# A decoder layer on one core: squares, the bias of the attention output, the experts' product and the last chunk's passes are rearranged

## The chip, the cores and the metric

The kernel runs on one NeuronCore of a Trainium2 chip. The metric is the device time of one launch, in microseconds (us). The core has a tensor engine for matmuls (PE, with PEld for its weight loads), a vector engine (DVE), a scalar engine (ACT), GpSimd (POOL) and a sync engine (SP), which here issues all DMAs. Each engine runs its own instruction list in order; semaphores tie them together. A later instruction on an engine can't pass one that waits.

## The reference

All arrays are float32: x is 4 x 1024 x 512, the context 4 x 64 x 512. One layer has three blocks, each added to its input and followed by a LayerNorm:

```python
# block 1: state-space mixer and gated MLP
h  = x + mamba(rmsnorm(x) * w1)      # in_proj 512->2048, conv of 4 taps, silu, x_proj,
                                     # dt = softplus(...), h[t] = exp(dt*A)*h[t-1] + dt*B*u (16 states),
                                     # y = (C.h + D*u) * silu(z), out_proj 1024->512
xn = rmsnorm(h) * w2
b1 = h + (silu(xn @ w1.T) * (xn @ w2.T)) @ w3.T          # width 2048
x  = layernorm(x + b1)
# block 2: cross attention to 64 context keys, 16 heads
scores = q.k / sqrt(32)
t = exp(clip(mlp(mean of scores, mean row maximum, mean variance of softmax)))   # per head, over the sequence
out = softmax(q.k / (2 t)) @ v
x = layernorm(x + out @ Wo.T + bo)
# block 3: a dense product with experts of low rank
base = x @ W.T + b
gate = softmax(x @ R.T), kept for its top 2 of 8 experts, rescaled to sum 1
h = x @ A.T                          # 8 experts x 16 = 128 columns
x = layernorm(x + base + (gate * h) @ B)
```

The temperature t of a batch needs statistics over its whole sequence of 1024, so the attention proper of a batch can only begin when both of its halves have passed the first scores.

## The kernel before, in words

The 4 sequences are cut into 8 chunks of 512 tokens (c = 0 to 7; an even chunk and the next odd one make a sequence). The work of a chunk is cut into units, and five streams of units are laid over each other:

- **m, the mixer.** Its front for a chunk: `turn_in` (normalise and transpose the input), `conv` (input product and convolution, 8 blocks), `proj`, the first `dt` and softplus steps. Its scan: 64 steps; in each, GpSimd multiplies by B (L992) and later by C (L1002) on 128x1024 elements, ACT computes two decays (L1049), DVE runs two scans (L1339), and the sum over states goes to PE (L1644, half of it to DVE). After the scan come `gate`, `out` (the output product, 32 matmuls, L1589), `ht` (residual, squares for the second norm), `rms` and `turn_out` (normalised and transposed into the tile `fT`, L1600).
- **l**, the gate branch z and the later dt blocks.
- **y**, the dense part of block 1: `h`/`hv`/`hg`/`hm` (gated MLP, 16 blocks), `w3`, its LayerNorm, `turn` (transposed into `fT`) and `query`, which reads `fT`.
- **s**, the statistics: `sc1` (scores of 128 tokens and 8 heads, L1677), `mx` (row maximum, DVE L1428), `e1` (8 exponentials, ACT L1220, then a square L1224), `sq` (DVE L1434), `ent`; at an odd chunk `mean`, `mlp`, `clip`, `temper`. There are 8 of these groups per chunk.
- **x**, the pass of a chunk through blocks 2 and 3: four times (t = 0 to 3) `sc2`, `e2` (ACT L1254), `flip` (transposes, L1704, copied by ACT L1263), `val` (L1711), `on` (DVE L1481), `fl2` (L1717, ACT L1268), `wo` (output product, L1542, with a bias product L1723 ahead of it), `woa` (DVE L1485); then LayerNorm, `xturn` (L1656), `lg` and `hh` (16 small products each), `logits`/`top2` (a chain of small DVE operations), `gh`, `lora`, `base` with `fin` (L1740, L1542, L1753), `mixed`, LayerNorm.

Which unit comes next on an engine is decided when the program is built: `schedule` lists the units by a greedy walk with durations per unit (`m_parts`, `parts`), and among the heads of the five streams it takes the one that could start first; within a stream's look-ahead (`LOOK`) it takes the one with the smaller key, which is set by `PHASE`, one number per stream and chunk. `loads` places the DMAs on SP's list by the same walk. The list is fixed from then on: where the chip is later than the walk, engines wait in the written order. The 8 PSUM banks are shared: banks 0 to 3 serve the mixer and are given free for the other streams after the last `turn_out`, banks 4 to 7 serve the rest.

Three waits matter below. ACT writes the squares of `ht` into `fT`, which the `query` products of the chunk before read, so `ht` waits for all four of them. The weights of `wo` and of `base` share one tile pair `watt`, loaded in turns. And the passes of the chunks are one list: no unit of pass 7 stands ahead of any unit of pass 6 on any engine.

In the text, "scan c" runs on GpSimd from the first multiplication of chunk c (its `du`, L1017) to its last product by C, and "front c" from there to the start of scan c+1. Front 7 is what follows the last scan.

## Time and profile before

| | us |
|---|---|
| median of 3 timed runs | 4170.89 |
| lowest, highest | 4154.61, 4172.75 |
| time of the profiled execution | 4160.77 |
| its span | 4159.0 |
| PE busy | 3674.8 (88%) |
| POOL busy | 2441.5 (59%) |
| DVE busy | 2519.4 (61%) |
| ACT busy | 2165.4 (52%) |
| span after the last `out` begins (3574.8) | 584.2 |

Times in rows count from the start of the span. A busy PE isn't PE at its peak, since its matmuls are pipelined and their ends are modelled; one float32 matmul stands as two records. "<-" names what ended the idle time before an instruction. TensorE's granted clock stands as a share of 2.4 GHz, averaged over a stretch. A row on a stretch A:B gives its length and then the busy time (and number of instructions) of PE, PEld, DVE, ACT and POOL, the granted clock, the busy share of the DMA engines and GB/s.

### The profile page before, as it was taken

What the parts mean: (1) busy time and instruction counts of PE and PEld (TensorE: products, weight loads), DVE (VectorE), ACT (ScalarE), POOL (GpSimd) and SP (SyncE); (2) the same over time, 40 slices, a digit from 0 to 9 for tenths busy, and PEclk for the clock granted to TensorE, in tenths of its full rate; (3) what the DMA queues carried; (4) which work ended last, traced back from release to release, by engine and by line L of the source; (5) the groups of instructions that cost most, each with busy time, mean ns of one, the idle gap of its engine ahead of it and who ended that gap; (6) DMA issues with size and microseconds to landing.
All of it is one profiled execution on the core that took longest, in us unless ns stands there. A gap on an engine that the chain in (4) does not pass through costs nothing.

```text
span 4159.0 us, 36287 instructions
## 1 busy us (share of the span) xinstructions
PE 3674.8 (88%) x9984; PEld 1760.8 (42%) x9984; DVE 2519.4 (61%) x3286; ACT 2165.4 (52%) x5182; POOL 2441.5 (59%) x1069
## 2 busy tenths in 40 slices
PE   7667998899879999999989998999989998999477
PEld 3223443444334445544434345554334434554244
DVE  4884678567746886168755887158774787222211
ACT  5543544554555455565456547455466457340543
POOL 3884599559954995049963997029981998100000
PEclk9889999899989999999989999999989999999788
DMA  4433344335433442235433442125432443112000
GB/s 171 138 121 101 120 164 162 97 115 167 149 106 117 158 156 74 86 112 168 152 111 104 157 159 97 66 83 187 152 128 82 157 162 119 49 46 91 11 31 21
DMA packets 221268, 483.19 MB, mean 116 GB/s; under 512 B 31884, under 2 KB 32268, under 8 KB 220812
## 3 DMA queue, kind: packets, MB, share of 16 engines
q1 hardware_dynamic: 221068, 480.87, 35.5%
q8 instruction: 83, 1.36, 0.1%
q14 instruction: 117, 0.96, 0.1%
HBM read 470.82 MB, written 9.96 MB: 116 GB/s over the span
## 4 chain that ended last, share of the span: by engine, by line
PE 58%; POOL 7%; ACT 6%; DVE 6%; issue 5%; POOLq 0%; DVEq 0%; ACTq 0%
PE ps L1542 32%; PE ps L1629 7%; PE ps L1644 6%; PE ps L1589 5%; POOL hb L1002 5%; DVE hb L1339 2%; POOL hb L992 2%; PE ps L1677 2%; PE ps L1711 1%; ACT ps L1220 1%; ACT xw L1254 1%; PE ps L1723 1%; PE ps L1582 1%; PE ps L1753 1%; PE ps L1740 1%
## 5 line engine op out<-in xcount | busy, mean ns | idle before, releaser
L1002 POOL TENSOR_TENSOR hb<-hb,bc 128x1024 f32<-128x1024 f32 x512 | 1224.5, 2394 | 96.8 <-issue 53.2
L992 POOL TENSOR_TENSOR hb<-dtu,bc 128x1024 f32<-128x1024 f32 x481 | 1133.2, 2357 | 124.3 <-PE ps L1644 85.6
L1049 ACT ACTIVATE ps<-dt,a_neg 128x512 f32<-128x512 f32 x1024 | 697.3, 690 | 841.1 <-DVE hb L1339 834.8
L1542 PE MATMUL ps<-fT,wden 128*128 128x512 f32 x2304 | 1038.5, 599 | 10.0 <-DVE hm L1392 6.7
L1644 PE MATMUL ps<-hb,ident 128*128 128x512 f32 x1152 | 653.2, 668 | 255.7 <-POOL hb L1002 254.3
L1542 PEld LDWEIGHTS ps<-fT,wden 128*128 128x128 f32 x2304 | 441.1, 193 | 568.4 <-issue 568.1
L1339 DVE TENSOR_TENSOR_SCAN hb<-ps,state,hb 128x512 f32<-128x512 f32 x512 | 626.6, 1266 | 19.2 <-POOL hb L992 12.9
L1339 DVE TENSOR_TENSOR_SCAN hb<-ps,hb 128x512 f32<-128x512 f32 x512 | 593.8, 1204 | 17.0 <-POOL hb L992 12.4
L1355 DVE TENSOR_TENSOR ps<-ps,hb 128x512 f32<-128x512 f32 x448 | 311.0, 694 | 274.1 <-POOL hb L1002 273.3
L1629 PE MATMUL ps<-wden,hm 128*128 128x512 f32 x1024 | 469.7, 606 | 1.5 <-DVE res L1402 1.5
L1542 PE MATMUL ps<-xnT,wmix 128*128 128x512 f32 x1024 | 456.9, 595 | 13.8 <-ACT xnT L1073 7.8
L1644 PEld LDWEIGHTS ps<-hb,ident 128*128 128x128 f32 x1152 | 218.1, 205 | 590.0 <-POOL hb L1002 401.1
L1017 POOL TENSOR_TENSOR dtu<-dt,u 128x1024 f32<-128x1024 f32 x32 | 75.4, 2358 | 629.5 <-issue 559.6
L1629 PEld LDWEIGHTS ps<-wden,hm 128*128 128x128 f32 x1024 | 198.9, 195 | 258.6 <-issue 247.0
L1542 PEld LDWEIGHTS ps<-xnT,wmix 128*128 128x128 f32 x1024 | 193.7, 191 | 251.8 <-issue 251.5
L1025 POOL TENSOR_TENSOR res<-bc,res 128x512 f32<-128x512 f32 x32 | 39.5, 1266 | 319.9 <-DVE bc L1376 319.9
L1589 PE MATMUL ps<-wmix,u 128*128 128x512 f32 x512 | 221.4, 593 | 5.4 <-DVE u L1361 5.3
L1254 ACT ACTIVATE xw<-ps,nm,ftv 128x64 f32<-128x64 f32 x512 | 199.2, 421 | 20.4 <-PE ps L1677 20.4
L1306 DVE SCALAR_TENSOR_TENSOR hb<-hb,cols 128x512 f32<-128x512 f32 x192 | 143.9, 750 | 36.5 <-ACT hb L1092 31.9
L1402 DVE TENSOR_TENSOR res<-ps,res 128x512 f32<-128x512 f32 x128 | 86.7, 680 | 114.9 <-PE ps L1629 114.3
L1171 ACT ACTIVATE hm<-ps 128x512 f32<-128x512 f32 x128 | 75.0, 587 | 153.7 <-PE ps L1542 96.4
L1589 PEld LDWEIGHTS ps<-wmix,u 128*128 128x128 f32 x512 | 96.9, 190 | 128.7 <-issue 128.7
(197 smaller groups left out, 3980.5 us busy)
## 6 DMA issues: line engine op xcount, KB each, us to landing
bc<-bc_dram SPq DMA_DIRECT2D x1024, 256.0 KB, 3.6
wden<-in_w SPq DMA_DIRECT2D x192, 512.0 KB, 3.6
wmix<-in_w_mix SPq DMA_DIRECT2D x96, 512.0 KB, 3.7
watt<-in_w_qof SPq DMA_DIRECT2D x32, 512.0 KB, 4.3
xm<-in_x SPq DMA_DIRECT2D x8, 1024.0 KB, 5.5
res<-in_x SPq DMA_DIRECT2D x8, 1024.0 KB, 6.9
wden<-in_w_qof SPq DMA_DIRECT2D x16, 512.0 KB, 3.6
out<-res SPq DMA_DIRECT2D x8, 1024.0 KB, 4.3
```

Source lines behind the costliest of these rows:

```text
L992: TTn(hb[:, k % 4], dtu[:, :, :], bc[:, 0, k % 3].unsqueeze(1).broadcast_to([P, 2, CH]), ALU.mult).then_inc(s.s1_ready, 1)
L1002: TTn(hb[:, k % 4], hb[:, k % 4], bc[:, 1, k % 3].unsqueeze(1).broadcast_to([P, 2, CH]), ALU.mult).then_inc(s.s3_done, 1)
L1049: A_(dst, dt[:, p % 2, jj], ACT.Exp, scale=a_neg[:, j, n:n + 1]).then_inc(full_of(key), 1)
L1254: ins = A_(eb[:, hh], bank[:, h], ACT.Exp, bias=nm2[:, TT * half + i, hh:hh + 1], scale=ftv[:, 0, hh:hh + 1], accum_out=den[:, 0, i % 2, h ...
L1306: ins = V.scalar_tensor_tensor(acc[:, j % 3], up[:, j % 2, tap:tap + CH], conv_w[:, j, tap:tap + 1], acc[:, j % 3], ALU.mult, ALU.add)
L1339: V.tensor_tensor_scan(hb[:, i % 4, jj], src, hb[:, i % 4, jj], first, ALU.mult, ALU.add).then_inc(free_of(key), 1)
L1355: V.tensor_tensor(ps[:, 2], ps[:, 2], hb[:, i % 4, 0], ALU.add).then_inc(s.sum_done, 1)
L1402: V.tensor_tensor(res[:, c % 3, tt], src, res[:, c % 3, tt], ALU.add).then_inc(free_of(key), 1)
L1542: ins = M(dst, a, b, start=start and n == 0, stop=stop and n == len(pairs) - 1)
L1589: ins = M(dst[t], u[:, j, t * P:(t + 1) * P], wo, start=j == 0, stop=j == JB - 1)
L1629: ins = M(dst, hm[:, f, tt * P:(tt + 1) * P], wi[:, (f % 2) * 512:(f % 2) * 512 + 512], start=f == 0, stop=f == FG - 1)
L1644: ins = M(dst, ident[:, :], hb[:, i % 4, jj], start=False, stop=n == NS - 1)
```

## The change

1. **Squares.** ACT writes them into `xnT` and no longer waits for the queries of the chunk before; that wait moves to `turn_out`, which writes `fT`.
2. **Last chunk.** The passes of chunk 7 become a stream of their own, `w`, so that its units may stand between those of pass 6. The `base` weights of passes 6 and 7 are loaded once into `u`, whose mixer data is no longer needed, and pass 7 uses the `wo` weights of pass 6. In those two passes all four `base` products stand ahead of `lora`.
3. **Experts.** `hh` is computed transposed: 4 matmuls with 512 moving columns in place of 16 with 128. So DVE first copies the gates out 16-fold (a new 128x512 copy), PE transposes them (`lora`), and `gh` multiplies the transposed product.
4. **Bias.** The bias product ahead of each `wo` (32 in all) is gone. GpSimd adds the bias to the residual in a new unit `bo`, 4 additions of 128x512 per chunk; `bo` of chunk c-1 stands behind `ht` of chunk c on GpSimd, and `woa` waits for it. One more constant is loaded at the start.
5. **Values.** The attention values have one buffer in place of two, with a semaphore of their own.
6. The planner's durations, waits, `PHASE` and `LOOK` are new, so that units move on every engine.

Cut to its core:

```diff
-    got = [("out", c, 0), ("ht", c, 0), ("ht", c, 1), ("ht", c, 2), ("ht", c, 3)]
+    got = [("out", c, 0), ("ht", c, 0), ("ht", c, 1), ("ht", c, 2), ("ht", c, 3)] + ([("bo", c - 1)] if c else [])
...
-        got += [("hh", c), ("gh", c), ("lora", c), ("base", c, 0)]
+        early = 0 if c < CHUNKS - 2 else 4
+        got += [("hh", c)] + [("base", c, t) for t in range(early)] + [("lora", c), ("gh", c)]
         for t in range(TT):
-            got += [("fin", c, t), ("mixed", c, t)] + ([("base", c, t + 1)] if t + 1 < TT else [])
+            got += ([("base", c, t)] if t >= early else []) + [("fin", c, t), ("mixed", c, t)]
...
+            part(ACT_, EV, mine(n), ("query", c - 1, KC - 1))
+    elif kind == "bo":
+        part(POOL, 5.2, ("turn", c, KC - 1))
     elif kind == "out":
         for p in range(PAIRS):
             part(PE, 8 * MM, ("gate", c, PAIRS - 1))
     elif kind == "ht":
         part(DVE, EV, ("out", c, 0), ("store", c - 3), late=7.0 if c > 2 else 0.0)
-        part(ACT_, 0.9, mine(0), ("query", c - 1, KC - 1))
+        part(ACT_, 0.9, mine(0))
...
-WORK = {"x": 176.0, "s": 103.0, "y": 304.0}
-PHASE = {'y': (6.12, 6.01, 6.206, 6.132, 6.127, 6.01, 6.132, 6.01), 's': (7.437, 6.89, 7.686, 6.881, 7.587, 6.627, 6.484, 6.736), 'x': (8.786, 7.926, 8.998, 8.055, 8.453, 7.926, 9.282, 7.057)}
+WORK = {"w": 176.0, "x": 176.0, "s": 103.0, "y": 304.0}
...
-        got[("wf", c)] = ("wo", c, TT - 1)
+        got[("wf", c)] = ("wo", c, TT - 1) if c < CHUNKS - 2 else ("out", CHUNKS - 1, 0)
...
-    streams = {"m": m_plan(), "l": l_plan(), "x": x_plan(), "s": s_plan(), "y": y_plan()}
+    streams = {"m": m_plan(), "l": l_plan(), "x": x_plan(range(CHUNKS - 1)), "w": x_plan((CHUNKS - 1,)), "s": s_plan(), "y": y_plan()}
...
-LOOK = {'m': 0.162, 'l': 0.065, 'x': 0.046, 'y': 0.288, 's': 0.3}
+LOOK = {'w': 0.05, 'm': 0.265, 'l': 0.167, 'x': 0, 'y': 0.277, 's': 0.3}
...
+        if c < CHUNKS - 1:
+            got.append((DONE[("fin", c - 1, TT - 1)] if c else 0.0, 2, ("wo_load", c)))
+            got.append((DONE[("wo", c, TT - 1) if c < CHUNKS - 2 else ("out", CHUNKS - 1, 0)], 2, ("wf_load", c)))
...
+    got.append((kept + 6, 2, ("v_load", 0)))
+    for b in range(1, BATCH):
+        got.append((DONE[("val", 2 * b - 1, TT - 1)], 2, ("v_load", b)))
...
-        vbd = sb("vbd", [P, 2, HEADS // 2, 2 * DK])
+        vbd = sb("vbd", [P, HEADS // 2, 2 * DK])
...
+        def gh_of(c):
+
+            g = hm[:, 0] if c == CHUNKS - 2 else xw[:, 0:512]
+            return g.rearrange("p (t c) -> p t c", t=TT)
+
+        def ghT_of(c):
+            return hm[:, 1] if c == CHUNKS - 2 else xw[:, 512:1024]
...
+                if c == CHUNKS - 2:
+                    filled(sp, ("out", CHUNKS - 1, TT - 1))
+                    for m in range(2):
+                        sp.dma_start(u[:, 2 * m:2 * m + 2].rearrange("p j l -> p (j l)"), A["w_qof"][4 + m]).then_inc(s.wu_in, 16)
+                    return
...
-                    filled(sp, ("val", 2 * b - 3, TT - 1))
                     sp.wait_ge(s.kb_sum, b - 1)
                 for q in range(4):
                     sp.dma_start(kbd[32 * q:32 * q + 32, r, :, q * KEYS:(q + 1) * KEYS],
                                  k_dram[b, :, 32 * q:32 * q + 32, :].rearrange("c p k -> p c k")
                                  ).then_inc(kv_in[r], 16)
+
+            def load_v(b):
+                sp.wait_ge(s.zeroed, 2)
+                if b:
+                    filled(sp, ("val", 2 * b - 1, TT - 1))
                 vv = v_dram[b].rearrange("k (a e d) -> k a e d", e=2, d=DK)
                 for e in range(2):
-                    sp.dma_start(vbd[64 * e:64 * e + 64, r, :, DK * e:DK * e + DK], vv[:, :, e, :]
-                                 ).then_inc(kv_in[r], 16)
+                    sp.dma_start(vbd[64 * e:64 * e + 64, :, DK * e:DK * e + DK], vv[:, :, e, :]).then_inc(v_in, 16)
...
+                elif kind == "bo":
+                    pool.wait_ge(s.const_in, 16 * CONSTS)
+                    for c4 in range(KC):
+                        filled(pool, ("tr", c, 0, c4))
+                    for t in range(TT):
+                        ins = TTn(res[:, c % 3, t], res[:, c % 3, t], bo_b[:, :], ALU.add)
+                    ins.then_inc(s.bo_in, 1)
...
-                    if i == 0 and c:
-
-                        for c4 in range(KC):
-                            filled(act, ("q", c - 1, c4))
-                    A_(fT[:, i], ht[:, i], ACT.Square, accum_out=smo[:, 0, i:i + 1]).then_inc(s.ss2_ready, 1)
+                    if c == CHUNKS - 1 and i == 0:
+                        filled(act, ("z", c, JB - 1))
+                    A_(xnT[:, i], ht[:, i], ACT.Square, accum_out=smo[:, 0, i:i + 1]).then_inc(s.ss2_ready, 1)
...
+                    for c4 in range(KC) if c else ():
+                        filled(act, ("q", c - 1, c4))
...
+                    dve.wait_ge(s.bo_in, c + 1)
...
-                        V.tensor_tensor(gates, G1, each(gmax[:, :]), ALU.mult).then_inc(free_of(("lg", c)), 1)
+                        ch.link(V.tensor_tensor(gates, G1, each(gmax[:, :]), ALU.mult))
+                        V.tensor_copy(gh_of(c).rearrange("p t (e r) -> p t e r", e=EXPERTS), bcast(gates, RANK)
+                                      ).then_inc(free_of(("lg", c)), 1)
                 elif kind == "gh":
                     key = ("hh", c)
-                    emptied(dve, ("lg", c))
-                    h = filled(dve, key).rearrange("p (t e r) -> p t e r", t=TT, e=EXPERTS)
-                    V.tensor_tensor(gh.rearrange("p t (e r) -> p t e r", e=EXPERTS), h, bcast(gate[:, 2], RANK), ALU.mult
-                                    ).then_inc(free_of(key), 1)
+                    emptied(dve, ("lora", c))
+                    V.tensor_tensor(ghT_of(c), filled(dve, key), ghT_of(c), ALU.mult).then_inc(free_of(key), 1)
...
-                    M(dst, e64[:, :], w_dt[:, 0:512], start=True, stop=False)
-                    group(dst, [(oT[:, c4 * P:(c4 + 1) * P], wo[c4 // 2][:, c4 % 2]) for c4 in range(KC)], start=False
-                          ).then_inc(full_of(unit), 1)
-                elif kind in ("lg", "hh"):
+                    group(dst, [(oT[:, c4 * P:(c4 + 1) * P], wo[c4 // 2][:, c4 % 2]) for c4 in range(KC)]).then_inc(full_of(unit), 1)
+                elif kind == "lg":
                     for c4 in range(KC):
                         emptied(pe, ("tr", c, 1, c4))
                     dst = take(pe, unit)
-                    wide, at_ = (EXPERTS, 0) if kind == "lg" else (P, EXPERTS)
                     for t in range(TT):
                         T = TT * half + t
-                        ins = group(dst[:, t * wide:(t + 1) * wide],
-                                    [(qT[:, ci, T * P:(T + 1) * P], w_ra[:, ci, at_:at_ + wide]) for ci in range(KC)])
+                        ins = group(dst[:, t * EXPERTS:(t + 1) * EXPERTS],
+                                    [(qT[:, ci, T * P:(T + 1) * P], w_ra[:, ci, 0:EXPERTS]) for ci in range(KC)])
                     ins.then_inc(full_of(unit), 1)
+                elif kind == "hh":
+                    group(take(pe, unit), [(w_ra[:, ci, EXPERTS:RA], qT[:, ci, half * CH:(half + 1) * CH]) for ci in range(KC)]
...
+                    if c < CHUNKS - 2:
+                        wb = x_in(pe, 2 * c + 1)
+                    else:
+                        pe.wait_ge(s.wu_in, 32)
+                        wb = [u[:, 2 * m:2 * m + 2].rearrange("p j (c d) -> p (j c) d", d=DM) for m in range(2)]
...
-                    emptied(pe, ("hh", c))
+                    emptied(pe, ("lg", c))
                     for t in range(TT):
-                        ins = turn(dst[:, t * P:(t + 1) * P], gh[:, t], ident[:, :])
+                        ins = turn(dst[:, t * P:(t + 1) * P], gh_of(c)[:, t], ident[:, :])
...
-                        emptied(pe, ("lora", c))
-                    M(ps[:, USE[key][0]], ghT[:, i * P:(i + 1) * P], w_b[:, :], start=False, stop=True
+                        emptied(pe, ("hh", c))
```

`CONSTS` goes from 14 to 15, the tile `bo_b` (128x512) and the semaphores `bo_in`, `wu_in` and `v_in` are added, and the waits for `val`, `fl2` and `wo` in the first of the four steps are now also made against the pass before.

Three places on PE show what the new tables do. The first is behind `out` of chunk 5, between scans 5 and 6. L1589 is `out`, L1559 `turn_in` of chunk 6 (L1624 and L1594 after); L1704, L1717 and L1711 are flips and values, L1677 scores, L1542 with fT the queries, with watt the attention's output product. Before:

```order
L1589 MATMUL ps<-wmix,u 128x512 x32
L1704 MATMUL ps<-ident,xw 128x128 x8
L1677 MATMUL ps<-kbd,qT 128x256 x2
L1711 MATMUL ps<-vbd,xw 128x64 x8
L1677 MATMUL ps<-kbd,qT 128x256 x2
L1542 MATMUL ps<-fT,wden 128x512 x4
L1717 MATMUL ps<-ident,xw 128x128 x4
L1542 MATMUL ps<-fT,wden 128x512 x4
L1723 MATMUL ps<-w_dt,e 128x512
L1542 MATMUL ps<-watt,xw 128x512 x4
L1704 MATMUL ps<-ident,xw 128x128 x8
L1677 MATMUL ps<-kbd,qT 128x256 x2
```

and now:

```order
L1624 MATMUL ps<-wmix,u 128x512 x32
L1739 MATMUL ps<-ident,xw 128x128 x8
L1712 MATMUL ps<-kbd,qT 128x256 x2
L1747 MATMUL ps<-vbd,xw 128x64 x8
L1712 MATMUL ps<-kbd,qT 128x256 x4
L1753 MATMUL ps<-ident,xw 128x128 x4
L1712 MATMUL ps<-kbd,qT 128x256 x2
L1577 MATMUL ps<-watt,xw 128x512 x4
L1712 MATMUL ps<-kbd,qT 128x256 x2
L1739 MATMUL ps<-ident,xw 128x128 x8
L1712 MATMUL ps<-kbd,qT 128x256 x2
L1594 MATMUL ps<-dgi,xm 128x128 x16
```

Before, 28 rows stand between `out` and `turn_in`; now the three queries and one of the four attention steps stand ahead of `out`, and the last two steps behind `turn_in`.

The second is the end of the last chunk's MLP: L1629 is `w3`, L1677 with two or more matmuls the scores of the statistics, L1656 the transposes, L1542 with fT the MLP and the queries, L1687 the statistics' end. Before:

```order
L1629 MATMUL ps<-wden,hm 128x512 x16
L1542 MATMUL ps<-fT,wden 128x512 x24
L1677 MATMUL ps<-kbd,qT 128x256 x2
L1629 MATMUL ps<-wden,hm 128x512 x16
L1677 MATMUL ps<-kbd,qT 128x256 x4
L1656 MATMUL ps<-ident,res 128x128 x16
L1542 MATMUL ps<-fT,wden 128x512 x16
L1677 MATMUL ps<-kbd,qT 128x256 x16
```

and now (L1664 is `w3`, L1712 the scores, L1691 the transposes):

```order
L1664 MATMUL ps<-wden,hm 128x512 x16
L1577 MATMUL ps<-fT,wden 128x512 x24
L1712 MATMUL ps<-kbd,qT 128x256 x2
L1664 MATMUL ps<-wden,hm 128x512 x16
L1712 MATMUL ps<-kbd,qT 128x256 x14
L1691 MATMUL ps<-ident,res 128x128 x16
L1577 MATMUL ps<-fT,wden 128x512 x16
L1712 MATMUL ps<-kbd,qT 128x256 x16
```

Before, five of chunk 6's eight score groups stand further up, among the attention steps of pass 5; now all eight stand at the end, seven of them behind the last `w3`.

The third is where pass 6 ends. L1711 are values, L1656 transposes, L1542 with w_ra `lg` and `hh`, L1747 `lora`, the rest `base` and `fin`. Before:

```order
L1717 MATMUL ps<-ident,xw 128x128 x4
L1723 MATMUL ps<-w_dt,e 128x512
L1542 MATMUL ps<-watt,xw 128x512 x4
L1656 MATMUL ps<-ident,res 128x128 x16
L1542 MATMUL ps<-w_ra,qT 128x8 x16
L1542 MATMUL ps<-w_ra,qT 128x128 x16
L1747 MATMUL ps<-ident,xw 128x128 x4
L1740 MATMUL ps<-w_dt,e 128x512
L1542 MATMUL ps<-watt,qT 128x512 x4
L1753 MATMUL ps<-w_b,xw 128x512
L1740 MATMUL ps<-w_dt,e 128x512
L1542 MATMUL ps<-watt,qT 128x512 x4
```

and now (L1577 with watt and xw is `wo`, L1739 flips of pass 7, L1691 the transposes of pass 6, L1780 and L1577 with u `base` of pass 6):

```order
L1577 MATMUL ps<-watt,xw 128x512 x4
L1739 MATMUL ps<-ident,xw 128x128 x4
L1691 MATMUL ps<-ident,res 128x128 x16
L1739 MATMUL ps<-ident,xw 128x128 x4
L1712 MATMUL ps<-kbd,qT 128x256 x2
L1577 MATMUL ps<-w_ra,qT 128x8 x16
L1577 MATMUL ps<-qT,w_ra 128x512 x4
L1780 MATMUL ps<-w_dt,e 128x512
L1577 MATMUL ps<-u,qT 128x512 x4
L1780 MATMUL ps<-w_dt,e 128x512
L1577 MATMUL ps<-u,qT 128x512 x4
L1780 MATMUL ps<-w_dt,e 128x512
```

Before, pass 7 begins behind all of pass 6; now its first step runs between `wo` and the LayerNorm of pass 6, and `lg`, `hh` and all four `base` products of pass 6 stand inside its second step, ahead of that step's `val`.

## Rows read from the trace of the kernel before

**Rows 1.** The page, its first part: busy time by engine.

```profile
PE 3674.8 (88%) x9984; PEld 1760.8 (42%) x9984; DVE 2519.4 (61%) x3286; ACT 2165.4 (52%) x5182; POOL 2441.5 (59%) x1069
```

**Rows 2.** Stretches: length, busy time by engine, granted clock, DMA.

```profile
457.40:782.00 324.60, 284.78 (x633) 121.12 (x631) 253.49 (x284) 159.12 (x266) 305.76 (x132) 0.93 0.46 150
...
1301.00:1645.70 344.70, 318.70 (x899) 152.87 (x898) 264.96 (x332) 193.79 (x382) 306.12 (x132) 0.95 0.43 138
1645.70:1824.90 179.20, 169.37 (x594) 93.54 (x593) 57.31 (x116) 97.05 (x320) 4.96 (x5) 0.97 0.22 71
...
2151.20:2254.40 103.20, 93.41 (x269) 47.32 (x268) 46.16 (x76) 66.46 (x220) 4.92 (x4) 0.97 0.27 88
2254.40:2598.90 344.50, 317.87 (x897) 152.11 (x896) 265.88 (x331) 193.93 (x382) 306.08 (x132) 0.95 0.43 138
2598.90:2782.90 184.00, 174.22 (x595) 98.05 (x594) 57.42 (x116) 97.03 (x320) 4.95 (x5) 0.94 0.22 69
2782.90:3108.00 325.10, 301.40 (x690) 131.13 (x689) 253.76 (x307) 179.28 (x374) 305.87 (x132) 0.95 0.47 154
...
3210.70:3553.80 343.10, 318.56 (x901) 152.79 (x900) 266.76 (x331) 191.33 (x373) 306.04 (x132) 0.96 0.43 139
```

**Rows 3.** Timeline of PE around the `out` of chunks 4 and 5.

```profile
2154.61 27.70 PE L1589 MATMUL ps<-wmix,u 128*128 128x512 f32 x64 [0.91 <-DVE u L1361]
2191.09 5.83 PE L1559 MATMUL ps<-dgi,xm 128*128 128x128 f32 x32 [5.33 <-ACT dgi L1069]
...
2621.34 27.63 PE L1589 MATMUL ps<-wmix,u 128*128 128x512 f32 x64
...
2696.21 3.79 PE L1559 MATMUL ps<-dgi,xm 128*128 128x128 f32 x32
```

**Rows 4.** The chain that ended last: bias, four matmuls, `lg` with `hh`.

```profile
3628.63 0.86 PE ps L1723 x2
3629.49 3.43 PE ps L1542 x8
...
4008.51 10.65 PE ps L1542 x64
```

**Rows 5.** Stretches after the last `out` begins, columns as in rows 2.

```profile
3574.80:3861.00 286.20, 283.10 (x838) 145.49 (x837) 63.04 (x124) 92.27 (x317) 4.94 (x4) 0.98 0.19 65
...
3861.00:3892.50 31.50, 21.18 (x65) 12.07 (x65) 7.94 (x19) 16.35 (x54) 0.00 (x0) 0.89 0.06 17
3892.50:3941.90 49.40, 9.95 (x68) 8.30 (x67) 14.33 (x33) 30.74 (x151) 0.00 (x0) 0.60 0.00 0
3941.90:3997.00 55.10, 45.37 (x180) 29.21 (x179) 6.13 (x12) 33.15 (x141) 0.00 (x0) 0.84 0.00 1
3997.00:4048.60 51.60, 37.27 (x140) 24.70 (x140) 14.49 (x49) 12.22 (x19) 0.00 (x0) 0.84 0.12 41
4048.60:4102.40 53.80, 42.02 (x176) 26.33 (x176) 5.84 (x11) 34.45 (x142) 0.00 (x0) 0.84 0.05 20
4102.40:4159.00 56.60, 35.55 (x133) 23.18 (x132) 14.78 (x49) 12.19 (x18) 0.00 (x0) 0.81 0.10 37
```

**Rows 6.** Timeline of ACT: first and last statistics group of chunk 7.

```profile
3892.54 0.21 ACT L1216 ACTIVATE nm<-mxs 128x8 f32<-128x8 f32 x1 [2.12 <-DVE mxs L1428]
...
3926.35 0.21 ACT L1216 ACTIVATE nm<-mxs 128x8 f32<-128x8 f32 x1 [1.35 <-DVE mxs L1428]
```

**Rows 7.** Timeline of DVE: `woa` of two steps of pass 6.

```profile
3962.14 0.69 DVE L1485 TENSOR_TENSOR res<-ps,res 128x512 f32<-128x512 f32 x1 [6.80 <-PE ps L1542]
...
3972.86 0.69 DVE L1485 TENSOR_TENSOR res<-ps,res 128x512 f32<-128x512 f32 x1 [6.05 <-PE ps L1542]
```

**Rows 8.** Groups by line and shape: additions on GpSimd.

```profile
L1025 POOL TENSOR_TENSOR res<-bc,res 128x512 f32<-128x512 f32 x32 | 39.5, 1266 | 319.9 <-DVE bc L1376 319.9
```

**Rows 9.** DVE's multiplications in scan 0: least, median, most ns.

```profile
L1346 DVE TENSOR_TENSOR hb<-dtu,bc x31: 1198/2035/3411, 83.0 to 350.9; 128x1024 f32<-128x1024 f32 x31
```

**Rows 10.** The page, DMA issues: a row spread over 128 partitions.

```profile
bc<-bc_dram SPq DMA_DIRECT2D x1024, 256.0 KB, 3.6
```

76 lines of the change are left out of this document (40 added, 36 removed).

## The prediction, made before the changed kernel had run

> **What bounds the kernel now.** I read the busy times first: PE 88%, no other engine above 61% [rows 1]. An average hides stages, so I cut the span at the mixer's borders, where GpSimd starts and stops its steps [rows 2]. In each scan GpSimd is busy for 306 us. Scans 1 and 6 last 324.6 and 325.1 us, so GpSimd bounds them. Scans 3, 5 and 7, in which PE also does most of an attention pass, last 343 to 345 us with PE busy for 318: there PE's written order makes GpSimd wait for its sums. Fronts come in two kinds. Front 4 takes 103.2 us with PE busy for 93.4. Fronts 3 and 5 take 179.2 and 184.0 with PE busy for 169.4 and 174.2: they carry another pass, ahead of the mixer on PE. The timeline shows it: `turn_in` starts 8.8 us after `out` ends in front 4 (2154.61 + 27.70 to 2191.09), but 47.2 us after it in front 5 (2621.34 + 27.63 to 2696.21) [rows 3].
>
> After the last `out` begins, 584.2 us remain [rows 5]: 286.2 bound by PE (283.1 busy); 31.5 of LayerNorm and queries; 49.4 of statistics, in which PE works for 10; pass 6 with 55.1 for its four attention steps and 51.6 for the rest; pass 7 with 53.8 and 56.6. In these last four PE is busy for 37 to 45 us each, ACT for 12 to 34. No engine bounds them; a chain does. One attention step takes 10.7 us (`woa` at 3962.14 and 3972.86 [rows 7]), because its flips stand behind the `wo` of the step before and each link waits for the last.
>
> **The change part by part.** Prices of PE: a bias matmul takes 0.86 us, four matmuls of 512 columns 3.43, and `lg` with `hh`, 32 small products, 10.65, so half of it, 5.3, for `hh` [rows 4].
>
> *Bias and experts.* Each chunk loses 4 x 0.86 = 3.4 us of bias and 5.3 - 3.4 = 1.9 of `hh`, together 5.3 of PE. Five passes lie before the last `out`, so 26.5 us of PE work go there. GpSimd gains four additions of 1.27 us [rows 8], 5.1 per chunk. They stand right behind `ht`, where GpSimd idles for some 60 us until the next scan (its 4.92 busy of 103.2 in front 4 is `ht` alone [rows 2]): nothing on the path. If that cover were gone, 6 x 5.1 = 31 us. The new copy of the gates is one DVE operation per chunk, as wide as `woa` at 0.69 [rows 7]; DVE is busy for 61% of the span, and in the two last passes the four `base` products run meanwhile: nothing.
>
> *Fronts.* Front 3 has, besides 1.9 for `hh` and three bias groups (2.6), three queries (10.3) and one attention step (about 9.5 with its bias, by the prices above and the small products) fewer: 24 us, and PE is busy for 169 of its 179, so -24. In front 5 `turn_in` moves up past two steps and the queries: about 16 us instead of 47.2 behind `out`. The path behind it took 2254.40 - 2191.09 = 63.3 us in front 4 and 86.7 in front 5; with two attention steps still woven in I take 75, and 12 ahead of `out`. 12 + 27.6 + 16 + 75 is 131, and with some waiting 134: -50.
>
> *Scans.* What left the fronts is in the scans. Counting units at the prices above: scan 3 gets 15 us of PE work more, scan 5 15 more (both net of the bias), scan 6 18.6 more (the rest of pass 3, 20 us of `base` in one block between two sums, against MLP blocks that moved into front 5), scan 7 5.3 less. Nothing in the trace shows these orders, so I bound the price of 1 us of PE work moved into a scan. From below 0: scan 1 with 285 busy and scan 6 with 301 last equally long. From the rows nearest to it: scan 6 to scan 5 adds 16.5 busy and 19.4 of length, 1.2 per us. Scans 3 and 5 are past the bend, scan 6 stands just before it. I take 1: +49, and -5 for scan 7. Together with the fronts -24 - 50 + 49 - 5 = -30; ends: -79 and, at 1.5 per us, -5.
>
> *Front 7 up to the last `w3`.* PE-bound, so work counts: bias 3.4, `hh` 1.9, five score groups moved behind it (0.88 each by PE's 0.86 for the same number of columns, 4.4). -10, with 3 us of idle time as the other bound: -7 to -13. Here the squares no longer wait for the last query. That is worth little beyond this: PE was idle for 3.1 of 286.2 us, so the wait was covered by other products. The same holds for the other fronts.
>
> *Statistics of chunk 6.* The part of the change that costs. One group of statistics takes 4.83 us ((3926.35 - 3892.54)/7 [rows 6]), since maximum, exponentials, square and sum go to and fro between DVE and ACT. Before, five of the eight ran beside the attention steps of pass 5, which cost nothing. Now seven start behind the last `w3`. Between there and the end of the queries (31.5 us) about four fit, as ACT also has 16 us of its own work there less what it already did for two groups; flips of the transposes wait behind them and delay the queries by 2. The other four are 3.7 x 4.83 = 18, so chunk 7's statistics start 20 us later: +20. Bounds: 0 if they all fitted, 5 x 4.83 = 24 if none of the moved ones did.
>
> *Last passes.* Pass 6's four steps lose a bias each and share ACT with the first exponentials of pass 7: 55.1 - 3.4 + 1.7 = 53.4. Then, from its last `wo`: the first step of pass 7 (10.7); a second step that takes PE's block of pass 6, `xturn` 3.4 (as many columns as four matmuls of 512), `lg` 5.3, `hh` 3.4, `base` 17.2, `fin` 3.4, so about 45; and two steps of some 11.5 (9.9 without the bias, and ACT's scaling and table changes between). 10.6 + 45 + 23 = 78.6. The end is as before but for 1: 55.5. Sum 187.5 against 217.1: -30. Bounds: 0, if the block of pass 6 cost as much as its LayerNorm chain did (51.6 + 53.8 = 105.4 for both), and -51.6, if all of it were hidden.
>
> *The rest.* One more constant, 3.6 us as a lone transfer [rows 10], shares the queues with the others: +1, at most +3.6. The values in one buffer are needed only at the next sequence's first step: 0.
>
> Sum: -30 - 10 + 20 - 30 + 1 = -49, from 4160.8 to 4112 for an execution like the profiled one. The median of the timed runs stands 10.1 above that execution; I put in half and forecast 4118.
>
> **A rule against the change.** DVE's multiplication of two SBUF operands in scan 0 takes 1.20 us alone, but 2.04 in the median and up to 3.41 beside GpSimd's products [rows 9]: one waits for the other. The Trainium skill, "SBUF — State Buffer", section "SBUF: two separate sides", says that such a DVE operation and a GpSimd operation take one shared port pair in turn, each for the whole instruction; by that rule the trace agrees. New here are eight DVE copies within SBUF, four or more of them in scans, and 32 GpSimd additions. By rows 9 a collision costs at most 3.41 - 1.20 = 2.2 us: eight copies give 18 us, and the additions, which stand ahead of the convolution's taps, none. I leave it out of the sum and keep it as a rival.
>
> **The rivals.**
> - *The moved work isn't absorbed.* A 20 us block between two sums outlasts the four buffers that GpSimd works ahead (4 steps of 306/64 = 4.8 us, 19 us), and scans 3 and 5 now hold queries too. Scan 7 already ends so. At 1.6 to 1.8 per us the scans give +78 to +88 instead of +49: 4150.
> - *Pass 7 stands behind pass 6's block.* If its second step takes 65 instead of 45: 4138. For it: PE's order is fixed; against it: that step's own chain is only 10.
> - *Port waits*, as above, all eight and in the path: 4136.
> - *More than forecast.* Scan 6 takes its 18.6 us within its 24 us of idle PE, and front 5 goes to front 4's length: 4085.
> - *Slower than before.* One mechanism: GpSimd's products stop while PE does attention blocks in scans 3, 5 and 6. The other terms add up to -98 (-24, -50, -5, -10, +20, -30, +1); it decides from 98/49 = 2.0 us per us moved. At 2.5 the sum is +24: 4190. For it: the waits of the flips for ACT's exponentials stop PE as well, which a count of work doesn't contain. Against it: the 1.2 of the nearest rows.
>
> **How the numbers follow.** Forecast 4118 with its own range of 4098 to 4140: 0.58. Moved work not absorbed, 4150: 0.16. Pass 7 behind the block, 4138: 0.08. Port waits, 4136: 0.05. More, 4085: 0.07. Slower: 0.06. The range that holds 8 in 10 is 4085 to 4155. Less than 0.5%, 21 us, can't be told from no change. Faster means below 4150: 0.58 + 0.08 + 0.05 + 0.07 and a third of the 0.16, 0.83; the same 0.11, and slower 0.06.
>
> **What would show it.** Front 5 near 134 us with `turn_in` about 16 behind `out`; front 3 near 155; scans 3 and 5 near 360, scan 6 near 343, scan 7 near 338; the even fronts and scans 1, 2 and 4 unchanged; the last `out` beginning near 3545; 276 us from there to the last `w3`; chunk 7's first statistics 51 us behind it (31.5 before); then 49 to the first exponentials of pass 6, and 187 from there to the end, with one step of pass 7 of about 45 us. I am wrong if scan 6 grows by more than 30, if the statistics of chunk 6 cost nothing, or if the last two passes together save less than 15.

## The result and the profile after the change

The changed kernel takes 4145.32 us in the median of 8 runs (4136.56 to 4146.62), the kernel before 4167.0 in 8 runs beside it; the ratio is 0.9947 (95% interval 0.9935 to 0.9958). It is faster by 22 us, 0.5%, less than half of the 49 in the prediction's sum. The profiled executions differ by 17.9 us in span (4141.1 against 4159.0).

The page's busy times (span, then each engine's busy time and share) answer to [rows 1]: GpSimd has the additions, PE has lost only 1% and is still the busiest.

```profile
span 4141.1 us, 35899 instructions
PE 3648.7 (88%) x9728; PEld 1712.2 (41%) x9728; DVE 2527.0 (61%) x3294; ACT 2173.9 (52%) x5187; POOL 2481.8 (60%) x1101
```

The stretches of scans and fronts, with the columns of [rows 2]: scan 3, front 3, scan 5, front 5, scan 6, scan 7.

```profile
1299.30:1678.20 378.90, 350.72 (x961) 165.31 (x961) 273.82 (x347) 212.24 (x437) 306.18 (x132) 0.95 0.40 132
1678.20:1823.50 145.30, 133.79 (x475) 72.97 (x475) 54.43 (x107) 88.09 (x304) 9.87 (x9) 0.96 0.22 72
2256.50:2634.00 377.50, 349.99 (x962) 164.92 (x961) 273.82 (x347) 212.42 (x437) 306.15 (x132) 0.96 0.41 132
2634.00:2758.10 124.10, 113.99 (x395) 61.62 (x394) 43.49 (x67) 78.97 (x274) 9.87 (x9) 0.97 0.22 74
2758.10:3110.10 352.00, 324.08 (x762) 141.86 (x760) 266.21 (x342) 184.01 (x368) 306.23 (x132) 0.93 0.44 144
3212.60:3564.00 351.40, 321.66 (x878) 151.19 (x877) 269.48 (x333) 191.30 (x373) 306.35 (x132) 0.95 0.41 136
```

Against [rows 2] the fronts fell by 33.9 and 59.9 us, and the scans grew by 34.2, 33.0, 26.9 and 8.3. PE's busy time tells the same: 35.6 and 60.2 us left the two fronts, 32.0, 32.1, 22.7 and 3.1 arrived in the scans. The last `out` begins at 3580.84, 6 us later than before, where the prediction had it 30 earlier.

Behind it the stretches are: from the last `out` to the last `w3`; from there to the sums of chunk 7's statistics; from there to the end. In the kernel before, whose `out` begins at 3574.65 and whose sums at 3935.27, the same three took 286.4, 74.3 and 223.7 us. The first row here is that of the sums before (L1687), the others are the three stretches now:

```profile
3935.27 0.94 PE L1687 MATMUL ps<-ones_t,sta 128*3 128x1 f32 x32 [37.45 <-DVE sta L1457]
3580.80:3850.30 269.50, 268.99 (x786) 132.95 (x785) 56.77 (x115) 74.74 (x225) 9.85 (x8) 1.00 0.22 73
3850.30:3945.30 95.00, 35.59 (x108) 21.36 (x108) 27.66 (x56) 59.82 (x288) 4.93 (x4) 0.68 0.02 6
3945.30:4141.10 195.80, 152.35 (x606) 91.96 (x606) 42.93 (x127) 94.49 (x325) 0.00 (x0) 0.86 0.03 11
```

So +6.2 up to the last `out`, then -16.9, +20.7 and -27.9. Behind the last `out` the forecast (-10, +20, -30) holds for the two later stretches and is 7 us short of what the first one saved; before the last `out` it fails.

### The profile page after: what moved, and what is told of

The parts are those of the page before. It is cut to its first block, busy times and chain, and to the rows that moved or that the text cites. A ratio compares the mean times of both kernels' runs of the same rounds, so it can differ in the third digit from the quotient of the medians.

```text
span 4141.1 us, 35899 instructions
## 1 busy us (share of the span) xinstructions
PE 3648.7 (88%) x9728; PEld 1712.2 (41%) x9728; DVE 2527.0 (61%) x3294; ACT 2173.9 (52%) x5187; POOL 2481.8 (60%) x1101
## 4 chain that ended last, share of the span: by engine, by line
PE 56%; POOL 7%; ACT 7%; DVE 6%; issue 5%; POOLq 0%; DVEq 0%; ACTq 0%
PE ps L1577 31%; PE ps L1664 7%; PE ps L1679 6%; POOL hb L1027 5%; PE ps L1624 5%; DVE hb L1373 2%; POOL hb L1017 2%; PE ps L1712 1%; ACT xw L1288 1%; PE ps L1747 1%; ACT ps L1252 1%; PE ps L1617 1%; PE ps L1793 1%; PE ps L1780 1%; PE ps L1594 1%
## 5 line engine op out<-in xcount | busy, mean ns | idle before, releaser
L1577 PE MATMUL ps<-fT,wden 128*128 128x512 f32 x2304 | 1042.7, 601 | 16.1 <-DVE hm L1426 6.7
L1577 PEld LDWEIGHTS ps<-fT,wden 128*128 128x128 f32 x2304 | 442.0, 193 | 577.5 <-issue 573.4
L1373 DVE TENSOR_TENSOR_SCAN hb<-ps,hb 128x512 f32<-128x512 f32 x512 | 593.6, 1204 | 12.5 <-POOL hb L1017 9.0
L1664 PE MATMUL ps<-wden,hm 128*128 128x512 f32 x1024 | 470.5, 606 | 2.1 <-DVE res L1436 1.9
L1577 PE MATMUL ps<-xnT,wmix 128*128 128x512 f32 x1024 | 456.7, 596 | 13.6 <-ACT xnT L1105 8.2
L1664 PEld LDWEIGHTS ps<-wden,hm 128*128 128x128 f32 x1024 | 198.7, 195 | 260.2 <-issue 246.8
L1577 PEld LDWEIGHTS ps<-xnT,wmix 128*128 128x128 f32 x1024 | 193.9, 191 | 253.6 <-issue 253.3
L1624 PE MATMUL ps<-wmix,u 128*128 128x512 f32 x512 | 221.4, 593 | 6.1 <-DVE u L1395 6.1
L1288 ACT ACTIVATE xw<-ps,nm,ftv 128x64 f32<-128x64 f32 x512 | 199.3, 421 | 17.0 <-PE ps L1712 16.7
L1053 POOL TENSOR_TENSOR res<-res,bo_b 128x512 f32<-128x512 f32 x32 | 39.5, 1270 | 241.8 <-PE ps L1691 241.8
```

The source lines that it names most:

```text
L1288: ins = A_(eb[:, hh], bank[:, h], ACT.Exp, bias=nm2[:, TT * half + i, hh:hh + 1], scale=ftv[:, 0, hh:hh + 1], accum_out=den[:, 0, i % 2, h ...
L1373: V.tensor_tensor_scan(hb[:, i % 4, jj], src, hb[:, i % 4, jj], first, ALU.mult, ALU.add).then_inc(free_of(key), 1)
L1577: ins = M(dst, a, b, start=start and n == 0, stop=stop and n == len(pairs) - 1)
L1624: ins = M(dst[t], u[:, j, t * P:(t + 1) * P], wo, start=j == 0, stop=j == JB - 1)
L1664: ins = M(dst, hm[:, f, tt * P:(tt + 1) * P], wi[:, (f % 2) * 512:(f % 2) * 512 + 512], start=f == 0, stop=f == FG - 1)
```

## The experiments

Times are medians where a ratio to the kernel before stands beside them. "Period n" is the time from the start of scan n's first `du` on GpSimd to that of scan n+1 (period 7: to the last `out`).

**1. The new instructions in the old order.** Only what the planner orders the work by is changed: the tables, PE's costs and the wait that it counts for the squares are those of the kernel before, and the last chunk keeps its own list. The traces show the same order of PE's products as before up to the end of the statistics, the bias and `hh` aside. Three lines of the edit, the tables shortened:

```
-PHASE = {... 'y': (6.039, 6.01, 6.125, ...), 'x': (8.713, 8.394, 8.925, ...)}
+PHASE = {... 'y': (6.12, 6.01, 6.206, ...), 'x': (8.786, 7.926, 8.998, ...)}
-LOOK = {'w': 0.05, 'm': 0.265, 'l': 0.167, 'x': 0, 'y': 0.277, 's': 0.3}
+LOOK = {'m': 0.162, 'l': 0.065, 'x': 0.046, 'y': 0.288, 's': 0.3, 'w': 0.05}
-        part(PE, 4 * MM, ("fl2", *key), takes=(u,))
+        part(PE, 5 * MM, ("fl2", *key), takes=(u,))
```

> The changed kernel's instructions (bias on GpSimd, experts' product transposed, squares free, the last chunk's passes in their own list), but up to the last `out` and through the MLP behind it in the order of the kernel before. Theory A (the new order costs what the removed work saves): the periods from one scan's start to the next keep the lengths of before less the bias, the last `out` begins at 3555 to 3565 us (3574.8 before, 3580.8 after), chunk 6's statistics stay early, so chunk 7's begin about 33 us behind the last `w3`, and the tail keeps its 28: about 4110, 1.2% below before. Rival B (the order is innocent; the new instructions lengthen the scans themselves, by GpSimd's additions, the copy on DVE or the waits of the flips): the last `out` begins near 3580 here too, and the time is about 4130.

Measured: 4108.35 us, ratio 0.9864 (0.9846 to 0.9882), 37 us less than the changed kernel. The last `out` begins at 3560.39. The periods 3 to 7, first of the changed kernel, then of this one (columns as above):

```profile
1299.30:1823.50 524.20, 484.51 (x1434) 238.28 (x1434) 328.25 (x453) 300.33 (x740) 316.05 (x140) 0.96 0.35 115
1823.50:2256.50 433.00, 396.49 (x950) 178.19 (x949) 299.28 (x379) 239.90 (x557) 315.98 (x141) 0.95 0.41 136
2256.50:2758.10 501.60, 463.98 (x1354) 226.54 (x1354) 317.31 (x413) 291.39 (x710) 316.02 (x141) 0.96 0.36 118
2758.10:3212.60 454.50, 417.68 (x1031) 189.29 (x1030) 312.46 (x418) 250.67 (x587) 316.08 (x140) 0.94 0.39 130
3212.60:3580.80 368.20, 338.46 (x921) 159.35 (x920) 275.85 (x348) 193.13 (x377) 306.35 (x132) 0.95 0.40 132
```

```profile
1304.20:1825.10 520.90, 484.04 (x1427) 236.60 (x1426) 323.39 (x449) 290.90 (x702) 316.03 (x141) 0.95 0.36 116
1825.10:2255.00 429.90, 396.97 (x958) 178.86 (x957) 299.83 (x383) 245.91 (x592) 315.74 (x140) 0.95 0.42 137
2255.00:2770.70 515.70, 478.52 (x1427) 234.43 (x1426) 325.40 (x449) 290.81 (x702) 315.92 (x141) 0.96 0.36 117
2770.70:3200.60 429.90, 396.80 (x958) 178.76 (x957) 299.74 (x383) 245.74 (x592) 315.84 (x140) 0.95 0.41 135
3200.60:3560.40 359.80, 334.00 (x922) 156.13 (x921) 276.28 (x348) 191.38 (x374) 306.09 (x132) 0.96 0.42 135
```

The sum of the five is 2281.5 us in the new order and 2256.2 in the old one: the same instructions take 25.3 us longer, 10.8 of it as busy time of PE and 14.5 as waits. Single traces vary: experiments 2 and 7 have PE's order of the changed kernel in these periods and took 2288.1 and 2278.1, experiments 8 and 9 (its first kernel) have the old one and took 2256.0 and 2256.2. So the order costs 22 to 32 us there. The new order gains 14.1 in period 5 and loses 24.6 in period 6, 8.4 in period 7 and 6.4 in periods 3 and 4. Period 6 varies in the new order: it took 447.6 to 457.6 us in the seven traces with the new tables, some of which have other products in it (the longest 10.3 us more), always far above 429.9. Theory A holds; the order, and not the new instructions, cost most of the gain.

A part of the 10.8 us of busy time has a name: the pair `lg` and `hh`. These are its rows in periods 3 to 7 (`hh` first), of the kernel before, the changed one and this one:

```profile
L1542 PE MATMUL ps<-w_ra,qT 128*128 128x128 f32 x160 | 30.1, 375 | 0.0
L1542 PE MATMUL ps<-w_ra,qT 128*128 128x8 f32 x160 | 24.9, 297 | 1.3 <-ACT qT L1198 1.2
L1577 PE MATMUL ps<-qT,w_ra 128*128 128x512 f32 x40 | 29.8, 914 | 0.0
L1577 PE MATMUL ps<-w_ra,qT 128*128 128x8 f32 x160 | 22.4, 281 | 0.1
L1577 PE MATMUL ps<-qT,w_ra 128*128 128x512 f32 x40 | 26.8, 831 | 0.0
L1577 PE MATMUL ps<-w_ra,qT 128*128 128x8 f32 x160 | 18.7, 257 | 1.8 <-ACT qT L1230 1.8
```

The pair took 55.0 us, then 52.2, and 45.5 in the old order. In the changed kernel `lg` runs at a granted clock of 0.74 to 0.93 in these five passes, in this one at 0.95 to 1.00. So 6.7 of the 10.8 us are the pair at the lower clock (5.0 and 8.6 in the traces of experiments 7 and 2).

**2. Chunk 6's statistics early.** One rule in the planner: their score groups may be taken as soon as they are ready (the ends of the lines are left out).

```
-                    rank = (max(t, at[e] + LOOK[name]), ...)
+                    look = 0.05 if name == 's' and queue[e][name][place[e][name][0]][0][1] == CHUNKS - 2 else LOOK[name]
+                    rank = (max(t, at[e] + look), ...)
```

> The changed kernel with one edit in the planner: the eight score groups of chunk 6's statistics are taken as soon as they are ready, so all stand ahead of the last `w3`. Theory A (they cost 20 us behind the last `w3` because nothing hides their to and fro there): chunk 7's statistics begin 30 to 34 us behind the last `w3` instead of 52, the stretch from `out` to the last `w3` grows by the 7 groups' 6 us and some waiting, net -10 to -14: about 4133. Rival B (PE waits for each group's buffers as long in the MLP as behind it): the stretch from `out` grows by 20 and the time stays at 4145.

Measured: 4133.17 us, ratio 0.9924 (0.9909 to 0.9939), 12 less than the changed kernel. The stretch behind the last `w3` fell from 95.0 to 72.4, that ahead of it grew from 269.5 to 282.0 (second and first row; the third is the end, which is the changed kernel's):

```profile
3587.70:3869.70 282.00, 278.08 (x813) 138.50 (x811) 66.40 (x132) 97.31 (x351) 9.86 (x8) 0.99 0.21 70
3869.70:3942.10 72.40, 24.71 (x82) 15.31 (x82) 17.84 (x39) 36.98 (x162) 4.93 (x4) 0.72 0.02 7
3942.10:4137.70 195.60, 152.31 (x606) 91.94 (x606) 42.92 (x127) 94.44 (x325) 0.00 (x0) 0.86 0.03 11
```

Theory A holds: 22.6 us of to and fro lay bare behind the last `w3`, as the term of +20 said; hidden beside the MLP they cost 12.5. Up to the last `out` PE's order is that of the changed kernel, and yet this trace gets there 6.9 us later: a difference of that size between single traces says nothing.

**3. The bias back on PE.**

```
+                    M(dst, e64[:, :], w_dt[:, 0:512], start=True, stop=False)
...
-                    for t in range(TT):
-                        ins = TTn(res[:, c % 3, t], res[:, c % 3, t], bo_b[:, :], ALU.add)
...
-                    dve.wait_ge(s.bo_in, c + 1)
```

> The changed kernel with the bias of `wo` back on PE (32 products) and GpSimd's 32 additions left out; the order is the same. By the count of the prediction 32 x 0.86 = 27.5 us of PE work come back, 17 of them ahead of the last `out`. Theory A (the bias product stood where PE waits for ACT's copy of `fl2` or for a slot of its own, so only part of it was on the path): +8 to +16, with the wait ahead of `wo` shorter by some. Rival B: full price, +22 to +27. Rival C (GpSimd's additions and the waits for them cost as much as they save): 0 or below.

Measured: 4171.77 us, ratio 1.0012 (1.0001 to 1.0024), 26.5 more than the changed kernel: 32 x 0.86 = 27.5 at nearly full price. My theory A was wrong, rival B right. The run puts the products back and takes the additions out at once, so 26.5 is the difference of the two. GpSimd's 32 additions, in its row of the changed kernel, stand in idle time:

```profile
L1053 POOL TENSOR_TENSOR res<-res,bo_b 128x512 f32<-128x512 f32 x32 | 39.5, 1270 | 241.8 <-PE ps L1691 241.8
```

**4. The experts' product ahead of the small one, in the new order and in the old.** In both kernels `lg` and `hh` change places on PE, and `hh` now also waits for the transposes that `lg` waited for.

```
+for n, u in enumerate(ORDER[PE]):
+    if u[0] == "lg" and ORDER[PE][n + 1][0] == "hh":
+        ORDER[PE][n + 1] = u
+        ORDER[PE][n] = ("hh", u[1])
```

> The changed kernel with PE's products `lg` and `hh` of each pass exchanged: the four products of 512 columns stand ahead of the 32 small ones. In the changed kernel they follow them and take 5.3 to 6.7 us at a granted clock of 0.55 to 0.68, against 3.68 at 1.00 in pass 5. Theory A (the clock falls with the small products before them): `hh` now takes 3.4 to 4.0 us in most passes, and what follows `lg` (the turns of the gates, the first `base`) takes 1 to 2 us more; net -1 per pass, -5 to -10 in all. Rival B (the clock falls already with the turns and their waits ahead of both): `hh` takes 5.5 or more as before, the time stays.

> The run with the old order again, with PE's products `lg` and `hh` exchanged. In the changed kernel's order the exchange cost about 10 us, although `hh` fell to 3.67: PE then waited 6 us for the gates in front of `lora`, which stands right behind the two products there. In the old order three sums of the mixer or two `dt` products and an MLP product stand between them and `lora`. Theory A (the half clock of `hh` was only hidden behind the wait for the gates): here the exchange saves 1.8 us (9.0 to 7.3) in each of passes 0 to 5 and 2 to 5 in passes 6 and 7, together 8 to 15: about 4097. Rival B (the lower clock only moves on to what follows): 4108 and no change; rival C: slower as in the other order, by 5 to 15.

Measured: 4160.18 us in the new order, ratio 0.9986 (0.9976 to 0.9996), and 4122.73 in the old one, ratio 0.9895 (0.9881 to 0.9908): about 15 and 14 us slower than without the exchange. PE's timeline in scan 5 (start, length, then the instructions, and in brackets the idle time ahead of them with its releaser) of the changed kernel and of the exchange in the new order:

```profile
2577.52 4.87 PE L1577 MATMUL ps<-w_ra,qT 128*128 128x8 f32 x32
2582.24 5.86 PE L1577 MATMUL ps<-qT,w_ra 128*128 128x512 f32 x8
2588.44 0.63 PE L1787 MATMUL ps<-ident,xw 128*128 128x128 f32 x4 [0.33 <-DVE xw L1559]
```

```profile
2588.00 3.67 PE L1581 MATMUL ps<-qT,w_ra 128*128 128x512 f32 x8
2591.51 3.63 PE L1581 MATMUL ps<-w_ra,qT 128*128 128x8 f32 x32
2601.19 1.09 PE L1793 MATMUL ps<-ident,xw 128*128 128x128 f32 x4 [6.05 <-DVE xw L1563]
```

The granted clock of the 512-column products is read from the stretches that hold them: in scan 5 of the changed kernel, behind the small products, and in pass 5 of it, where the small ones had run at full clock.

```profile
2582.20:2588.10 5.90, 5.90 (x9) 2.26 (x9) 4.75 (x25) 0.60 (x2) 0.00 (x0) 0.62 0.00 0
3701.10:3704.80 3.70, 3.70 (x11) 1.79 (x11) 2.81 (x15) 0.18 (x1) 0.00 (x0) 1.00 0.02 4
```

At 0.62, so for the most part at the lower level of 1.2 GHz, the four products take 5.86 us; at 1.00 (2.4 GHz) they take 3.68. The Trainium skill, "TensorE: Matmul & The Clock Gate", section "What's actually happening", says that "the default state is throttled, and activity releases the throttle"; the trace agrees in so far as the level goes with what PE did before, for with `hh` first it takes 3.67. A busy PE was not enough: in scan 5 of the changed kernel `lg` took 4.87 us without a pause at 0.74, and `hh` came behind it at 0.62. Nor does the order of the pair alone decide: in pass 5 `lg` takes 3.63 us at 1.00 both in the changed kernel and in experiment 1, but `hh` behind it 3.68 at 1.00 there and 5.38 at 0.68 here. What else decides is not shown.

The faster `hh` gained nothing. What PE needs next are the turned gates, and DVE's chain to them starts at the end of `lg`. In both kernels `lora` starts 6.05 us behind the end of `lg`: in the changed one (2588.44 - 2582.39) the slow `hh` fills that time, after the exchange (2601.19 - 2595.14) nothing does. From the start of the pair to `lora` it is 10.9 us without the exchange and 13.2 with it. In the old order the mixer's sums stand there too, and from the end of `lg` to `lora` it takes 8.0 us with and without the exchange, so that `lora` comes 15.5 us behind the start of the pair instead of 11.8. Rival C was right in the old order. In the new one the time of `hh` came out as theory A had it and the total did not: it forecast -5 to -10. Both forecasts of a gain had overlooked that the exchange makes the gates late.

**5. Ten microseconds more of PE work in the middle of a scan.**

```
+                    if c in (0, 2, 3, 5, 6) and 8 <= i < 14:
+                        M(dst, wi[:, m * KC * P:(m * KC + 1) * P], fT[:, 0], start=True, stop=True)
```

> The changed kernel with 12 products of 512 columns more (the first product of 12 MLP groups is done twice, 10.3 us of PE work) in the middle of each of scans 1, 3, 4, 6 and 7; scans 2 and 5 stay. It measures the price of 1 us of PE work in a scan by itself, over the period from one scan's start to the next. The prediction's rule: 0 in scan 1 and 4 (GpSimd busy for 306 of 321 to 325 us), about 1 in scans 3, 6 and 7. The rival of the prediction (work put into a scan isn't absorbed): 1.6 to 2, so +16 to +20 in scans 3, 6 and 7. Theory A now (from the fourth chunk on a period is PE's busy time plus a constant 33 to 38 us): +10 in periods 3, 4, 6 and 7 alike, 0 to 10 in period 1.

Measured: 4196.27 us in its single run, 51 more than the changed kernel for 51.5 us of products. By period, against the changed kernel's trace: +12.0 in period 1, +15.5 in 3, +11.1 in 4, +3.1 in 6 and +13.6 in 7; -0.8 and +0.1 in the untouched periods 2 and 5. Period 6 is the one that varies; period 3 took 524.2, 524.3 and 530.4 in the three traces with the order of the changed kernel, so its 15.5 may be 9. Period 1 of this kernel and of the changed one:

```profile
461.20:888.90 427.70, 384.17 (x914) 169.10 (x913) 295.11 (x348) 220.19 (x458) 315.77 (x141) 0.95 0.42 132
```

```profile
459.30:875.00 415.70, 371.84 (x890) 163.50 (x889) 290.90 (x348) 220.32 (x457) 315.65 (x140) 0.95 0.41 136
```

The two rows differ by 12 us in PE's busy time (10.3 of it by the products' price) and by 12 in length, in a scan in which GpSimd was busy for 306 of 321 us. The prediction's reading of scans 1 and 6, "so GpSimd bounds them", was wrong for scan 1, and for scan 4, to which I had carried it in the text above: extra PE work there isn't free. For scan 6 this run doesn't settle it, as its period varies by more than the 3.1.

**6. The same ten microseconds in the last quarter.** There PE is idle the most.

```
+                    for _ in range(3 if c in (0, 1, 3, 4) else 0):
+                        M(dst, wq[0][:, 0, i * P:(i + 1) * P], fT[:, 0], start=True, stop=True)
```

> The changed kernel with three products of 512 columns more in front of each of the 16 products groups of `query` of chunks 0, 1, 3 and 4: 12 products, 10.3 us of PE work, now in the last quarter of scans 1, 2, 4 (behind sums 51 to 57) and, for chunk 4, of scan 5 (behind sums 59 to 62, beside an attention pass). In the middle of a scan the same 10.3 us cost 11 to 15 us, in scan 1 too. Theory A (a scan is limited by PE in its first three quarters and by GpSimd in its last, unless an attention pass fills it): 0 to 3 us in scans 1, 2 and 4, and 9 to 13 in scan 5. Rival B (a period is PE's busy time plus a constant, wherever the work stands): 10 in each of periods 1, 2, 4 and 5.

Measured: 4184.91 us in its single run, 40 more than the changed kernel for 41.2 us of products. By period +12.4, +12.2, +10.6 and +10.0 us in periods 1, 2, 4 and 5 (and +2.8, -6.9 and +0.3 in the untouched 3, 6 and 7). Rival B was right, theory A wrong. A stretch of 20 us in scan 1 beside the queries, of this kernel and of the changed one at the same place:

```profile
741.00:761.00 20.00, 20.00 (x51) 9.94 (x50) 9.90 (x12) 11.06 (x24) 15.73 (x7) 0.91 0.30 92
```

```profile
739.30:759.30 20.00, 19.20 (x52) 8.84 (x50) 11.14 (x14) 14.87 (x29) 20.00 (x10) 0.98 0.28 97
```

GpSimd falls from 20.00 to 15.73 us. As the products were placed, three ahead of each query, a query of seven products and a sum takes 6.9 us (8 x 0.86) on PE, longer than GpSimd's step of 4.8, and PE's idle time elsewhere in the scan doesn't help, since its order is fixed.

**7. One list again.** `"x": x_plan(range(CHUNKS))`, with the phase of before (7.057) for the last chunk.

> The changed kernel with the last chunk's passes back in one list with the others, nothing else moved up to the last `w3`. Theory A (the list of its own is worth the 28 us that the trace shows behind the first exponentials of pass 6): +20 to +30, about 4170, the same up to the statistics. Rival B (the tail got shorter by the bias and the early `base` products): +5 or less.

Measured: 4166.78 us, ratio 1.0003 (0.9993 to 1.0013), 21.5 more than the changed kernel; the stretch from the statistics' sums to the end is 219.5 us instead of 195.8, and the last `out` begins within 0.8 us of the changed kernel's:

```profile
3944.50:4164.00 219.50, 159.95 (x606) 99.17 (x606) 43.01 (x127) 95.56 (x325) 0.00 (x0) 0.81 0.03 10
```

Theory A holds.

**8. The squares wait again**, on top of experiment 1.

```
+                    for c4 in range(KC) if i == 0 and c else ():
+                        filled(act, ("q", c - 1, c4))
```

> The run with the old order, with the squares of the mixer's output waiting for the last query product again. Theory A (the wait was covered by other products on PE): 0 to +3 us, the time stays at 4108. Rival B (ACT's wait delayed the turns of each front): +2 us or more in each of 7 fronts, 4122 or more.

Measured: 4103.46 us, ratio 0.9853 (0.9835 to 0.9871), which overlaps experiment 1's, with the starts and ends of all scans in its trace within 0.5 us of it. The wait cost nothing that can be seen.

**9. Two kernels that beat both.** Experiment 1 with `lg` and `hh` exchanged in the last two passes alone, and that with other numbers in the tables, which put pass 5 ahead of the last `out`.

```
+    if u[0] == "lg" and ORDER[PE][n + 1][0] == "hh" and u[1] > CHUNKS - 3:
```

> The run with the old order, with `lg` and `hh` exchanged in the last two passes alone, where four `base` products stand between them and `lora` and hide the gates. With the exchange in all passes the stretch from the last mean's sums to the end took 191.7 us against 198.4, and the scans with an attention pass 4 to 9 us more each. Theory A: -4 to -7 against the old order, near 4102, with everything up to the last `w3` as there. Rival B (the saving came from elsewhere): 4108.

> As the run before, with numbers of the table that the planner's own times make 8 us shorter (4257.1 against 4265.0 in its own count): pass 5 is done ahead of the last `out`. If the planner's times are as good for this as for the other orders, 4095; if PE's waits for GpSimd in scan 7 grow as they did with the block in scan 6 of the changed kernel, 4105 to 4120.

Measured: 4102.22 us, ratio 0.9854 (0.984 to 0.9867), and 4100.36, ratio 0.9847 (0.9833 to 0.9861). Both are some 1% below the changed kernel and can't be told from each other, nor in their medians from experiment 8. The end of the first is 190.3 us in its trace against 198.5 in experiment 1's; PE's order up to the last `w3` is as there, though this trace reaches it 6 us earlier:

```profile
3909.70:4100.00 190.30, 146.59 (x574) 89.21 (x574) 42.74 (x127) 94.58 (x324) 0.00 (x0) 0.88 0.03 12
```

In the second, period 7 grew by 67.4 us and the stretch from `out` to the last `w3` shrank by 65.6: pass 5 only changed its place.

## Why the prediction was wrong, step by step

- **The step that failed is *Scans*:** "I take 1: +49, and -5 for scan 7". These three scans got 94 us longer, not 49, and scan 7 8 longer instead of 5 shorter. Counted by PE's busy time the price was right: scans 3, 5 and 6 grew by 34.2, 33.0 and 26.9 us for 32.0, 32.1 and 22.7 us more of busy time, 1.07, 1.03 and 1.19 per us, and extra products cost about the same by themselves (experiments 5 and 6). The amount was wrong: 87 us arrived where I had 49, and 3 in scan 7 where I had 5 fewer. Part of the amount is work that I had not counted: the records of the three scans at their full-clock prices come to +30, +31 and +15 (an estimate; I had 15, 15 and 18.6); the rest is busy time above these prices. By that count scan 6 paid 1.8 per us (1.5 in experiment 2's trace), the other two 1.1.
- **Fronts.** Front 3 -33.9 instead of -24, front 5 -59.9 instead of -50; `turn_in` came 16.7 us behind the end of `out` (2642.13 + 27.63 to 2686.5), as forecast. I had drawn the border of a front at `out` in PE's order, and the trace draws it where GpSimd stops; some 10 us each changed sides, and that alone costs nothing. Front 4 took 5.2 more.
- **What the two have in common.** By my terms the five periods should have fallen by 30; they grew by 7.8. In the old order they fell by 17.5, where the bias and `hh` by my prices should have given 26.5. So about 9 us of the gap are there without the new order, and the other 29 are the order: I had it at -4 net, and it costs 25.3. It is the order that made scan 7 longer, too: in the old one it took 339.6 us, 3.5 less than before.
- **`hh`.** I took half of the 10.65 us of `lg` with `hh` for `hh`, and so 5.3 - 3.4 = 1.9 us per pass. In the five passes `hh` had taken 6.0 us each and `lg` 5.0. In the changed kernel the pair fell by 2.8 us in all: the four wide products at the lower clock cost nearly what the small ones had cost. In the old order it fell by 9.5, just what I had counted, but that was luck: 3.3 of it is `hh`, and 6.2 is `lg` at a higher clock, which is no term of mine. Both rest on a clock that I had left out.
- **The 9 us without the new order.** They are not the pair. PE's busy time in the five periods fell by 19.0 us from the kernel before to experiment 1 and its waits rose by 1.6, while pair and bias together gave 27.6: 9.5, and 22.8 of the bias products less 4.7 that `wo`'s own products took more. So other products, the same in number, took some 8 to 9 us longer. Why is open.
- **The bias.** Right, 3.4 us per chunk at full price (experiment 3), with GpSimd's additions, 1.25 to 1.28 us each, in its idle time.
- **Front 7 up to the last `w3`.** -16.9 instead of -10, outside my 7 to 13: moving seven score groups cost 12.5 us in experiment 2, 1.8 each, where I had 0.88, so the five gave 9 instead of 4.4 (an estimate); and pass 5's pair took 7.3 us instead of 10.7. **Statistics of chunk 6:** +20.7, forecast +20. **Last passes:** -27.9, forecast -30; one list accounts for 23.7 of it (experiment 7). **Squares:** nothing, as forecast. **Constant:** scan 0 begins at 73.3 instead of 73.7, so nothing instead of +1. So the forecast was missed ahead of the last `out`.
- **The rival "the moved work isn't absorbed"** gave 4150 and came nearest, and its mechanism is in the trace. In scan 6 the four `base` products stand in one block on PE from 2807.71 to 2828.40 without a sum between them, and GpSimd waits 14.55 us for the next sum; in scans 3 and 5 it waits for 14.1 us at one place each. In the old order no wait of GpSimd in scan 6 is longer than 3.2 us.

```profile
2830.75 2.37 POOL L1017 TENSOR_TENSOR hb<-dtu,bc 128x1024 f32<-128x1024 f32 x1 [14.55 <-PE ps L1679]
```

PE works meanwhile, though, and what the wait costs is small: PE's idle time in scan 6 rose from 23.7 to 27.9 us. So the price of 1.6 to 1.8 holds for scan 6 by my count of units, and for no scan by busy time.

- **Port waits.** They cost next to nothing. The copy of the gates took 0.43 us each time in experiment 1, and in the changed kernel in seven of eight passes, each time with GpSimd idle. Once, at 3545.42, GpSimd had begun a product at 3544.78, and the copy took 1.98 us and ended behind it, so 1.55 us were lost where the rival had 2.2. I had expected four or more of them beside products; that GpSimd stood idle at nearly all was luck.

```profile
L1559 DVE COPY xw<-gate x7: 426/426/1980, 1632.1 to 4105.6; 128x512 f32<-128x512 f32 x7
```

- **Sums and signs.** The rival "more than forecast" doesn't add up: 4118 less 18.6 for scan 6 and 31 for front 5 is 4068, not 4085; and 4112 with half of the 10.1 us is 4117. None of the three signs of being wrong appeared (scan 6 grew by 26.9, the limit was 30), and yet the forecast was wrong: scans 3 and 5, expected near 360 us and measured at 378.9 and 377.5, had no sign of their own.

The medians say the same: experiment 1 stands 56 us below the kernel before that ran beside it, and the changed kernel 37 above experiment 1 (28.4 in the traces, of which experiment 1's is the slowest of its four executions). That this comes out near the 22 measured is no proof, since both differences share a median. Of that, experiment 2 gives 12 to the late statistics.

What stays open is how the 25.3 us divide among the pieces that the new order moves. It isn't PE waiting more for GpSimd: ahead of the sums it waits less than in the old order. These rows are PE's sums and its value products in periods 3 to 7 (idle time and releaser at the end), of the changed kernel and of experiment 1:

```profile
L1679 PE MATMUL ps<-hb,ident 128*128 128x512 f32 x640 | 355.2, 645 | 92.5 <-POOL hb L1027 91.7
L1747 PE MATMUL ps<-vbd,xw 128*128 128x64 f32 x320 | 39.7, 278 | 7.2 <-ACT xw L1297 6.2 <-issue 1.0
```

```profile
L1679 PE MATMUL ps<-hb,ident 128*128 128x512 f32 x640 | 354.5, 644 | 99.2 <-POOL hb L1027 98.2
L1747 PE MATMUL ps<-vbd,xw 128*128 128x64 f32 x320 | 38.6, 274 | 2.5 <-ACT xw L1297 2.5
```

What rose are small waits for ACT and DVE: ahead of the values 7.2 us against 2.5, of the flips of the scores 6.7 against 4.9, of the flips of the attention (L1753) 3.6 against 0.4, of the MLP's and the queries' products 11.7 against 7.6, of the mixer's `proj` (L1610) 14.6 against 11.3. That fits steps of a pass that now stand closer behind each other, and the rival "slower than before" had named such waits, at a price far above the one measured. But no run moved one piece alone.

## What to carry to other kernels

- Where two engines hand work to each other through a short queue in a written order, neither "bounds" a stretch by its busy share. The price of work there is measured by adding some: 10.3 us of products cost 10 to 15.5 us in eight of nine places (one trace each), in scan 1 too, where GpSimd was 95% busy. And count moved work between borders that the trace has, not between borders in the program.
- Run new instructions in the old order before new numbers for the planner: here that is the faster kernel by 37 us, and the run that tells the two effects apart.
- Before a product is made shorter, look at what its engine waits for behind it. `hh` filled a wait for the gates; made fast and put first, it made the gates late.

## What the runs showed of the hardware that I had not expected

- Four products of 512 columns took 5.86 us at a granted clock of 0.62 behind 32 products of 8 columns, and 3.67 when they stood ahead of them. What PE did ahead of the slow ones were the small products, busy for 4.87 us without a pause at 0.74; ahead of the fast ones it did 16 transposes (3.58 us) and a sum (1.02 us), without a wait. Behind small products that had run at 1.00 they took 3.68 us in pass 5 of the changed kernel and 5.38 in passes 4, 5 and 6 of experiment 1.
- PE's idle time per period hardly moves with its work: 32.9 and 33.1 us in periods 4 and 6 of experiment 1, 34.1 and 33.5 of the kernel before, and 36.5 in period 4 of the changed one with and without the 10.3 us of products more.
- The DVE copy of the gates (128x512 within SBUF) took 0.43 us with GpSimd idle, in 15 of 16 cases of two traces, and 1.98 us when a product of GpSimd had begun 0.64 us ahead of it.
